# Expert rows scattered to fixed DRAM regions as each block is routed, and loaded from there by plain transfers

## What is computed

```python
def _L0_ffn_ref(hidden_states, gate_w, Wg, Wu, Wd, Sg, Su, Sd):
    x = hidden_states.reshape(-1, h)                     # 2048 x 128, after a layer norm
    logits = x @ gate_w                                  # 8 experts
    top_v, top_i = jax.lax.top_k(logits, K)              # K = 2
    top_p = jax.nn.softmax(top_v, axis=-1)
    combine = jnp.zeros((T, E), x.dtype).at[jnp.arange(T)[:, None], top_i].add(top_p)
    g = jnp.einsum('th,ehi->tei', x, Wg)                 # i = 352
    u = jnp.einsum('th,ehi->tei', x, Wu)
    d = jnp.einsum('tei,eih->teh', jax.nn.silu(g) * u, Wd)
    expert_out = jnp.einsum('te,teh->th', combine, d)
    shared = jax.nn.silu(x @ Sg) * (x @ Su) @ Sd         # width 176, every token
    return (expert_out + shared).reshape(b, s, h)
...
x = x + _L0_xattn_ref(_layernorm(x, axis=-1), ctx_2048, ...)
x = x + _L0_attn_ref(_layernorm(x, axis=-1), ...)
x = x + _L0_ffn_ref(_layernorm(x, axis=-1), ...)
```

## Time and profile before

| | us |
|---|---|
| median of 3 runs | 657.82 |
| lowest and highest | 650.55, 662.43 |
| the profiled execution, whole | 651.66 |
| its span (first to last instruction) | 649.9 |
| busy in it: PE, DVE, ACT, POOL | 519.3, 408.3, 342.2, 381.8 |

### The profile page before, as it was taken

How to read it: one execution, slowest core, us unless ns; L and a number is a source line. 1 busy time by engine, 2 the same in 40 slices (tenths; PEclk the granted TensorE clock), 3 DMA queues, 4 the chain that set the end, 5 groups by cost and what they waited for, 6 DMA issues and landing times. The chain is left out here.

```text
span 649.9 us, 14494 instructions
## 1 busy us (share of the span) xinstructions
PE 519.3 (80%) x4330; PEld 349.0 (54%) x4330; DVE 408.3 (63%) x784; ACT 342.2 (53%) x1022; POOL 381.8 (59%) x720
## 2 busy tenths in 40 slices
PE   3799999999999999359786996973375576967892
PEld 2467777777777777322222322331353465866792
DVE  7477887878778787642866838683748132333446
ACT  3688888888888887122307244243343233433440
POOL 4146666666666666274594876853554756656540
PEclk9989999999999999856889879998586779898997
DMA  9115562222222220000000000000110111111216
GB/s 219 48 53 170 162 169 83 73 78 68 80 73 73 74 64 26 2 0 0 1 1 0 0 2 1 0 1 0 32 33 2 35 39 45 46 38 45 42 34 194
DMA packets 57639, 34.15 MB, mean 53 GB/s; under 512 B 4298, under 2 KB 56356, under 8 KB 57604
## 3 DMA queue, kind: packets, MB, share of 16 engines
q1 hardware_dynamic: 55108, 28.60, 15.7%
q0 software_dynamic: 2496, 5.12, 2.9%
HBM read 29.05 MB, written 4.65 MB: 52 GB/s over the span
## 5 line engine op out<-in xcount | busy, mean ns | idle before, releaser
L571 ACT ACTIVATE probs<-psum,neg_max 128x289 f32<-128x289 f32 x256 | 125.8, 498 | 34.7 <-DVE neg_max L744 34.7
L744 DVE TENSOR_REDUCE neg_max<-psum 128x1 f32<-128x289 f32 (+1 forms) x192 | 95.4, 552 | 45.5 <-PE psum L677 45.5
L627 PE MATMUL psum<-ident,probs 128*128 128x128 f32 x512 | 83.0, 285 | 1.6 <-ACT probs L571 1.3
L627 PEld LDWEIGHTS psum<-ident,probs 128*128 128x128 f32 x512 | 59.4, 152 | 26.8 <-issue 24.7
L919 POOL TENSOR_TENSOR read<-recep,state 128x496 f32<-128x496 f32 x32 | 45.6, 1426 | 30.9 <-DVE state L1155 30.9
L1400 POOL DMA_INDIRECT y_rows<-x_sq,dest_row x39 | 38.3, 982 | 36.3 <-DVE x_sq L1719 29.4
L462 POOL TENSOR_TENSOR inv_spread<-quad_of,inv_sum 128x128 f32<-128x128 f32 x64 | 25.5, 398 | 56.5 <-DVE inv_sum L740 56.5
L677 PE MATMUL psum<-kT,q_heads 32*128 32x289 f32 x512 | 49.8, 458 | 0.8 <-ACT probs L571 0.8
L571 ACT ACTIVATION_READ_ACCUMULATOR probs<-psum,neg_max 128x1 f32 x256 | 50.5, 197 | 0.0
L1155 DVE TENSOR_TENSOR_SCAN state<-decay,kv 128x512 f32<-128x512 f32 x32 | 49.0, 1530 | 1.1
L1712 DVE TENSOR_TENSOR ex_hidden<-w_up,psum 128x352 f32<-128x352 f32 x39 | 20.3, 521 | 40.4 <-remote 19.9
(11 more groups left out here) (263 smaller groups left out, 1250.9 us busy)
## 6 DMA issues: line engine op xcount, KB each, us to landing
k_in<-in_ctx SPq DMA_DIRECT2D x64, 128.0 KB, 2.5
v_in<-in_ctx SPq DMA_DIRECT2D x64, 128.0 KB, 2.5
w_gate<-in_L_ffn_Wg SPq DMA_DIRECT2D x1, 1408.0 KB, 7.9
w_up<-in_L_ffn_Wu SPq DMA_DIRECT2D x1, 1408.0 KB, 7.0
x_res<-in_x SPq DMA_DIRECT2D x4, 256.0 KB, 3.7
v_own<-in_ctx SPq DMA_DIRECT2D x2, 512.0 KB, 7.2
w_down<-in_L_ffn_Wd SPq DMA_DIRECT2D x2, 512.0 KB, 5.0
x_rows<-x_cen SPq DMA_DIRECT2D x4, 256.0 KB, 2.3
```

Of the source, the lines that this page charges most:

```text
L571: last = nc.scalar.activation(probs_of(par, gr), bank[S_BANK[gr]][:, 0:KEYS], ACT.Exp, bias=neg_max[:, par, gr:gr + 1], accum_out=row_sum[ ...
L627: last = pe.transpose(bank[PT_BANK[h]][:, P * (2 * k + c):P * (2 * k + c) + P], probs_of(par, 2 * h + k)[:, P * c:P * c + P], ident[:])
L744: nc.vector.tensor_reduce(neg_max[:, par, start:end], psum[:, start:end, 0:KEYS], AX.X, ALU.max, negate=True).then_inc(s_max, 1)
```

## The change

`x_rows` becomes a DRAM tensor of 19328 rows of 130 numbers: 2048 rows for each of the 8 experts (for the last one the rest), so an expert's region starts at a known row. The two extra numbers are the row's destination in `y_rows` and its probability. During the time mixing SP fills all of it once with zeros from an SBUF tile `blank`. Each block is routed by itself as soon as its logits are there (`top_two`, `slots`, `places`), its running counts are kept in `taken`, and POOL scatters its rows straight into the regions: 8 indirect DMAs for each block, 32 in all (`rows_to_slots`). The one-hot inversion is gone. DVE makes two small tables of 39 entries: the expert of each tile and its first row. SP loads each tile with one plain transfer from a row number in a register, into NXS = 8 buffers. DVE computes each tile's destinations from the loaded rows (`destination`) and multiplies with the probability when it copies a tile out (`down_out`). The shared expert runs after the routing, its POOL steps are now DVE's, and its second product and the addition stand before the expert loop. At the end DVE adds whole blocks of 512 numbers in two instructions for each block.

```diff
+        x_rows = nc.dram_tensor("x_rows", (X_ROWS, ROW), F32, kind="Internal").ap()
+            @block.sync
+            def _(sp):
+                sp.wait_ge(s_blank_made, 1)
+                sp.dma_start(x_rows.rearrange("(j p) c -> p j c", p=P),
+                             blank[:].unsqueeze(1).broadcast_to([P, X_ROWS // P, ROW])).then_inc(s_blank, 16)
...
             @block.sync
             def _(sp):
-                for n in range(NB):
-                    tiles = slice(TPB * n, TPB * n + TPB)
-                    sp.wait_ge(s_ln_norm, NB * 2 + n + 1)
-                    sp.dma_start(x_rows_tiles[:, tiles, :], x_cen[:, tiles, :]).then_inc(s_rows_out, 16)
+                sp.wait_ge(s_table, 2)
+                sp.wait_ge(s_rows_in, 16 * TOP * NT)
+                row = []
+                for i in range(NTILE):
+                    if i % GROUP == 0:
+                        row += table_values(mybir.EngineType.SP, tile_row, i, X_ROWS - SLOTS)
+                    if i >= NXS:
+                        sp.wait_ge(s_ex_out, i - NXS + 1)
+                    sp.dma_start(xs[:, i % NXS, :], x_rows[bass.ds(row[i], SLOTS), :]).then_inc(s_xs[i % NXS], 16)
...
             def _(pool):
+                def rows_to_slots(n, some):
+                    if some[0] == 0:
+                        pool.wait_ge(s_rows_copied, n + 1)
+                        pool.wait_ge(s_top, ROUTE_STEPS * (n + 1))
+                    for k in some:
+                        for m in range(TOP):
+                            t_no = TPB * n + k
+                            g.indirect_dma_start(x_rows, bass.IndirectOffsetOnAxis(
+                                ap=slot_no[:, m, t_no:t_no + 1].bitcast(mybir.dt.uint32), axis=0),
+                                rows_out[:, m, t_no, :], None).then_inc(s_rows_in, 16)
...
-                pool.wait_ge(s_rows_out, 16 * NB)
-                pool.wait_ge(s_top, TOP_SOURCE)
-                for i in range(NXS):
-                    gather(i)
-                pool.wait_ge(s_top, TOP_DEST)
-                for i in range(NXS, NTILE):
-                    scatter(i - NXS)
-                    gather(i)
-                for i in range(NTILE - NXS, NTILE):
-                    scatter(i)
+                for i in range(NTILE):
+                    pool.wait_ge(s_dest, i + 1)
+                    pool.wait_ge(s_ex_out, i + 1)
+                    g.indirect_dma_start(y_rows, bass.IndirectOffsetOnAxis(ap=dest_row[:, i:i + 1].bitcast(mybir.dt.uint32), axis=0),
+                                         ys[:, i % NYS, :], None).then_inc(s_ys[i % NYS], 16)
...
             def _(v):
+                centre_rows(0)
+                centre_rows(1)
+                variance(0)
+                normalise_rows(0)
+                centre_rows(2)
+                variance(1)
+                normalise_rows(1)
+                top_two(0)
+                centre_rows(3)
+                variance(2)
+                normalise_rows(2)
+                slots(0)
+                top_two(1)
+                variance(3)
+                normalise_rows(3)
+                slots(1)
+                top_two(2)
+                slots(2)
+                top_two(3)
+                slots(3)
...
+                def destination(i):
+
+                    token = xs[:, i % NXS, C:C + 1]
+                    v.wait_ge(s_xs[i % NXS], 16 * (i // NXS + 1))
+                    step(nc.vector.scalar_tensor_tensor(spare_dest[:, i:i + 1], token, 0.0, spare_row[:, i:i + 1], ALU.is_equal, ALU.mult))
+                    nc.vector.tensor_tensor(dest_row[:, i:i + 1], spare_dest[:, i:i + 1], token, ALU.add).then_inc(s_dest, 1)
...
-                    nc.vector.tensor_copy(ys[:, i % NYS, :], Y_BANK[:, 0:C]).then_inc(s_ex_out, 1)
+                    nc.vector.tensor_scalar(ys[:, i % NYS, :], Y_BANK[:, 0:C], xs[:, i % NXS, C + 1:C + 2], None,
+                                            ALU.mult).then_inc(s_ex_out, 1)
```

More of the change, by code:

```diff
@@ L881, in _ @@
                 ln_gpsimd(pool, 1)
+                g.memset(blank[:], 0.0).then_inc(s_blank_made, 1)
                 g.memset(read[:], 0.0)
@@ L1389, in gather @@
[L1389 to L1398 removed]
+                rows_to_slots(0, (2, 3))
@@ L1548, in _ @@
                 turn_rows(0)
+                logits(0)
                 turn_rows(1)
-                logits(0)
-                shared_up(0)
-                turn_rows(2)
-                logits(1)
-                turn_rows(3)
-                logits(2)
-                logits(3)
-                shared_up(1)
-                counts()
-                shared_up(2)
-                for c in range(NCHUNK):
-                    inverse(c)
-                shared_up(3)
-                def owners(first):
-                    return nc.values_load_multi_w_load_instructions(
-                        tile_owner[0:1, first:min(first + GROUP, NTILE)], engines=(mybir.EngineType.PE,), min_val=0, max_val=E - 1,
-                        skip_runtime_bounds_check_because="a sum of at most E - 1 ones, clamped")[1]
+                logits(1)
@@ L1569, in turn_slots @@
+                places(0)
+                turn_rows(2)
+                logits(2)
+                places(1)
+                turn_rows(3)
+                logits(3)
+                places(2)
+                places(3)
+                shared_up(0)
+                for n in range(1, NB):
+                    shared_up(n)
+                    shared_down(n - 1)
+                shared_down(NB - 1)
                 def turn_slots(i):
@@ L1623, in _ @@
                         expert_down(i - 2, owner[i - 2] * DROW)
-                for n in range(NB):
-                    shared_down(n)
             @block.vector
             def _(v):
-                ln_vector(v, 2)
+                centre_rows, variance, normalise_rows = ln_parts(v, 2, None, lambda n: rows_out[:, 0, tiles_in(n), 0:C])
                 done = [0]
@@ L1653, in _ @@
-                step(nc.vector.tensor_reduce(second_rank[:], is_second[:], AX.X, ALU.max))
-                step(nc.vector.tensor_tensor(hot[:, 1], is_second[:], over_experts(second_rank), ALU.is_equal))
-                assert done[0] == TOP_SECOND_HOT
-                step(nc.vector.tensor_tensor(gap[:], second[:], best[:], ALU.subtract))
-                assert done[0] == TOP_GAP
-                v.wait_ge(s_counts, 1)
-                step(nc.vector.tensor_tensor_scan(reach[:].rearrange("p e t -> p (e t)"), segment[:].rearrange("p e t -> p (e t)"),
-                                                  TOTAL, 0.0, ALU.mult, ALU.add))
@@ new lines, in slots @@
+                def slots(n):
+                    ts = tiles_in(n)
+                    v.wait_ge(s_gap_exp, n + 1)
+                    step(nc.vector.tensor_scalar(gap_den[:, ts], gap_exp[:, ts], 1.0, None, ALU.add))
+                    step(nc.vector.reciprocal(rows_out[:, 0, ts, C + 1], gap_den[:, ts]))
+                    step(nc.vector.tensor_tensor(rows_out[:, 1, ts, C + 1], gap_exp[:, ts], rows_out[:, 0, ts, C + 1], ALU.mult))
+                    v.wait_ge(s_counts, n + 1)
+                    step(nc.vector.tensor_tensor(place[:, ts], PLACE[n], taken[:].unsqueeze(1).broadcast_to([P, TPB, E]), ALU.add))
+                    step(nc.vector.tensor_tensor(chosen[:], hot[:, :, ts], place[:, ts].unsqueeze(1).broadcast_to([P, TOP, TPB, E]),
+                                                 ALU.mult))
+                    step(nc.vector.tensor_tensor(taken[:], taken[:], COUNT[n], ALU.add))
+                    step(nc.vector.tensor_reduce(slot_no[:, :, ts], chosen[:], AX.X, ALU.max))
+                    assert done[0] == ROUTE_STEPS * (n + 1)
@@ L1694, in _ @@
[L1694 to L1698 removed]
+                nc.vector.tensor_copy(tile_owner[:, 0:NTILE], tile_expert[:]).then_inc(s_table, 1)
@@ new lines, in shared_add @@
+                def shared_add(n):
+                    v.wait_ge(s_sh_down, n + 1)
+                    rows = x_res[:, tiles_in(n), :]
+                    nc.vector.tensor_tensor(rows, bank[SH_DOWN[n % 2]].rearrange("p (t c) -> p t c", c=C), rows,
+                                            ALU.add).then_inc(s_sh_added, 1)
+                for n in range(NB):
+                    shared_low(n)
+                shared_hidden(0)
+                for n in range(1, NB):
+                    shared_hidden(n)
+                    shared_add(n - 1)
```

376 lines of the change are left out of this document (162 added, 214 removed).

## The result

The changed kernel takes 646.93 us (median), the kernel before 655.93 beside it: a ratio of 0.988, interval 0.985 to 0.991. The ratio leaves out the slower executions of each kernel, those over 1.5 per cent above its fastest. It is faster by 1.2 per cent, where 629 was forecast. The profiled execution of the changed kernel took 647.21 us, of which its span is 645.5.

A forecast was written before the change was run, and what follows sets the result against it. Bound: PE at 2.09 us a tile plus about one us of held-up signals under POOL's dense indirect DMAs. Start 12.8, loop -34.0, end -2.6 sum to -23.8: 651.66 becomes 627.9, plus one for the median, 629; range 616 to 656.

The forecast's parts named there:

- What bounds the loop: Expert loop before: PE at 2.09 us a tile plus about one us of held-up signals while POOL issues indirect DMAs densely.
- The loop: Expert loop, gathers on POOL replaced by SP loads: 86.1 us instead of 120.1, 34.0 us less.
- The two DVE steps for the destination: Expert loop: two added steps of 0.17 cost nothing while PE is the bound, at most 16 us otherwise.
- The end: From the last scatter on: bound by result loads, 647.3 against 649.9, 2.6 us less.
- The fill with zeros: In the time mixing: 10 MB, estimated at 50 us, with 180 us available.
- The start: Ahead of the expert loop: all 32 scatters must come first, so the first transpose is at 523.7, 12.8 us later.
- ends by 516 and is hidden under POOL's scatters: Shared expert ahead of the loop: starts near 496, 19.3 us of PE at full clock, through before the scatters.
- the theory of the loop: Expert loop: PE's signals held up about one us a tile while POOL issues indirect DMAs densely; POOL as cause not shown.
- The sum: Whole kernel: start, loop and end, 12.8 - 34.0 - 2.6 = -23.8 us, giving 627.9 on the profiled run.
- Rival 2: Late start: POOL and DVE in each other's way, or PE's signals held up under 32 scatters; 649 us, chance 0.17.
- Rival 1: Expert loop: hold-ups stay, from many small transfers in flight, 3.08 us a tile; 661.9 us, chance 0.17.
- Range and chances: Whole kernel: 616 to 656 us; faster by over two per cent 0.70, within 0.22, slower 0.08.

The follow-up runs named there:

- run 7: Kernel before with its 39 gathers on POOL replaced by 39 plain SP loads of fixed rows (output not the reference's): 611.9 us.
- run 12: Changed kernel with one more gather on POOL per tile of the expert loop, on a chip with the kernel before at 647.5: 690.3 us.
- run 13: Changed kernel with a POOL memset after each of the 32 scatters of rows, on a chip with the kernel before at 647.5: 647.6 us.
- run 10: Kernel before, unchanged, traced once more on a chip without late signals: 625.2 us.
- Run 11: Changed kernel, unchanged, on a chip with the kernel before at 625.2: 632.0 us, ratio 1.012 (1.008 to 1.017).
- run 5: Kernel before, unchanged, traced on a chip with late signals: 655.2 us in the profiled run, 660.8 as median of the runs beside.
- run 6: Changed kernel, unchanged, on a chip with the kernel before at 660.8: 648.0 us, ratio 0.990 (0.980 to 1.000).
- run 8: Changed kernel with two of the shared expert's four blocks ahead of the expert loop and two behind it: 638.5 us, ratio 0.972 (0.958 to 0.986).

## Why the prediction was wrong, step by step

**What bounds the loop: right for the chip, and half right as a cause.** PE at 2.09 us a tile plus held-up signals was what the earlier trace rows showed, and runs 7, 12 and 13 show that indirect DMAs close together on POOL bring them. But they do so on two of the eight chips met in runs 1 to 18 (and in the first traces, whose chip may be one of them). On the six others no trace has such a wait, and the one trace of the kernel before among them, run 10, is bound by POOL's pace of 2.56 us a tile for a scatter and a gather; its loop is 28 us shorter than the 123.2 of the late chip. No row of one trace could tell that.

**The loop: 34.0 forecast, 33.2 measured.** The two DVE steps for the destination cost nothing, SP's loads were there in time, and the pace was PE's from the second tile on.

**The end: 2.6 forecast, 2.4 measured. The fill with zeros:** 51.6 us to landing against an estimate of 50. That it is wholly hidden is not shown: the time mixing ends at 453.8 to 457.6 in the four traces without it and at 456.0 to 465.0 in the sixteen with it, medians 2.4 us apart.

**The start: 12.8 forecast, 31.2 measured; this step failed**, at the sentence that at full clock the shared expert "ends by 516 and is hidden under POOL's scatters". Of the 17.2 us that the first transpose came later behind the time mixing than forecast (84.3 against 67.1), the last scatter carries 0.5, the first load behind it 1.3 (4.4 against 3.15), and 15.4 lie between that load and the transpose (18.4 against 3.0), which is the shared expert still at work. It begins late and lasts long. The working has it from 496, 39.4 us behind the time mixing, and for 20 us; the trace has it from 508.0, 50.2 behind, and for 33.8 us, to 541.8. Run 11, on a prompt chip, has 41.3 and 20.9 (506.2 to 527.1). Between these two traces lie 8.9 and 12.9 us, and the waits for the unnamed releaser are 7.7 in routing and 7.1 and 5.9 in the shared expert. The granted clock is lower too (0.73 over the shared expert against 0.91), which makes PE's busy time in it 24.0 us instead of 20.1; how much of that lies beside the waits was not separated. The working priced the stretch as PE time alone, 19.3 us, and its hand-overs at nothing. I had read in the earlier trace rows that a signal of PE can be 4 us late beside POOL's descriptors at 0.94 plus 0.30 us, and then put a chain of hand-overs under 32 scatters at 0.98 plus 0.30, without carrying the reading over. Taken at its word, the theory of the loop foretold the failure of the start. On a prompt chip the step holds: 68.3 against 67.1. But there the loop's gain is 9.1 us (95.7 to 86.6) and not 34, since nothing was held up before either. The sum took its gain from a late chip and its cost from a prompt one. With both from one chip, and the time mixing left out, the three rows of the tables give 30.1 - 33.2 - 2.4 = -5.5 for the first traces, -8.8 for runs 5 and 6, and 14.1 - 9.1 - 1.7 = +3.3 for runs 10 and 11. The medians say -9.0 on the first chip and +6.7 on the prompt one; what these sums leave out is the end of the time mixing, which the change also touches by its fill with zeros; how much of its spread is the change's was not measured.

**Rival 2** gave 649 and the profiled run took 647.2. Its sum has a slip: from tables near 520 the working's own 19.3 us reach 539, not the 544 it uses, which makes the start 16 us later and the time 645. Of its two causes the one named in half a sentence, signals of PE held up under the scatters, was it; the one that carried the price, DVE and POOL in each other's way, did not occur. DVE's routing steps with two SBUF inputs take 0.19 us beside scatters and without them (the line of `is_second`, four blocks, minimum, median and maximum in ns):

```profile
L1634 DVE TENSOR_TENSOR is_second<-is_second,rank x4: 191/191/192, 470.6 to 493.9; 128x32 f32<-128x32 f32 x4
```

By the Trainium skill, page "SBUF — State Buffer", section "Who interferes with whom", a DVE instruction with two SBUF inputs contends with a GpSimd instruction that reads SBUF; the same section infers that `tensor_tensor` takes only the read side of the shared ports while descriptor generation needs the write side. This row agrees with the latter: the steps take no more time beside POOL's indirect DMAs. The right time with the wrong price is luck.

**Rival 1** (hold-ups stay in the loop) is refuted, with no such wait in the loop. **Range and chances:** 646.9 lies in the range. Faster by over 2 per cent had 0.70 and did not come; within 2 per cent had 0.22. The kinds of chips were in none of the cases.

**A version that beats both** exists for a late chip: two blocks ahead, 638.5 against 648.0 and 660.8. On a prompt chip none of mine beats the kernel before.

## What to carry to other kernels

When a stall in the kernel before is put down to a condition (here: indirect DMAs 1.3 us apart on POOL), look for every place where the change creates that condition anew, and price what lies there by its hand-overs, not by its busy time. A chain of hand-overs is cheap cover only where signals are prompt. Spacing the DMAs made it prompt on a late chip (run 13), but the later last scatter took the gain; moving half of the chain elsewhere did gain (run 8); fewer and longer pieces were not tried. And before a gain is read off one trace, time the kernel before on more than one chip: here the change is 1.0 to 1.2 per cent faster on one kind and 1.2 per cent slower on the other.

## What the runs showed of the hardware

- Chips differ in this. Eight chips were met in runs 1 to 18: on six the kernel before takes 625 to 628 us, on two 647 (one run) and 661; the first traces' 656 are of a chip without a number on record. Each was met once, so that a chip keeps its kind is not shown. POOL's indirect DMA takes 0.95 to 0.99 us (medians) on all.
- The traces have one more mark of the kind, apart from the waits: a median from issue to landing stands beside SP's loads of tiles in all eleven traces of the changed kernel and its versions on prompt chips (1.8 or 1.9 us) and in none of the five on late ones, not even in run 13, where nothing is late. Why the profile lacks it there no run shows.
- On a late chip, DVE and ACT wait up to 9.7 us (run 6, in routing) for signals of PE that are overdue by its recorded ends, while indirect DMAs are issued 1.27 us apart; at 1.89 us (run 13) and at 2.06 us (loop of runs 6, 8 and 13) no such wait was seen. Every such wait was of an instruction that waits for PE. The trace models the end of a product, so that the signal is late and not the product itself is a reading; for it speaks that PE starts later products meanwhile (513.33 in the timeline above). What in the chip delays them stays open, also whether it is POOL's writing of descriptors or the transfers themselves, since spacing thins out both.
